# Attention scores and weighted sums written to PSUM instead of SBUF, and the count of earlier tokens per expert formed by TensorE instead of VectorE

## The reference, cut to what matters

```
W = weight * mask[None, :, :]                       # (16, 5000, 128)
h = einsum('bg,egp->bep', x, W) + bias              # (64, 16, 128)

scores = einsum('bhqd,bhkd->bhqk', q, k) * scale    # 8 heads of 16 + 2 dims, 16 positions
attn   = softmax(where(causal, scores, min))
out    = einsum('bhqk,bhkd->bhqd', attn, v)         # then @ W_o.T, added to h

top_scores, top_idx = top_k(sigmoid(xf @ gate_w.T), 2)
pos = cumsum(one_hot(flat_e, 64))[..., flat_e] - 1  # place of a token in its expert's list
y   = (silu(buf @ w1) * (buf @ w3)) @ w2            # per expert; routed = sum of the two, weighted
```

## Time and profile before

| What | Value |
|---|---|
| median of 3 runs | 318.57 us (317.5 to 321.41) |
| the profiled execution's own time | 316.17 us |
| its span, first to last instruction | 314.3 us |
| mean granted TensorE clock | 0.823 |
| busy: PE / DVE / ACT / POOL | 191.5 / 214.3 / 61.9 / 171.6 us |

### The profile page before, as it was taken

How to read it: one execution, slowest core, us unless ns; L and a number is a source line. 1 busy time by engine, 2 the same in 40 slices (tenths; PEclk the granted TensorE clock), 3 DMA queues, 4 the chain that set the end, 5 groups by cost and what they waited for, 6 DMA issues and landing times.

```text
span 314.3 us, 5301 instructions
## 1 busy us (share of the span) xinstructions
PE 191.5 (61%) x2106; PEld 154.3 (49%) x2106; DVE 214.3 (68%) x427; ACT 61.9 (20%) x167; POOL 171.6 (55%) x120
## 2 busy tenths in 40 slices
PE   0177509986765775774893693667177648999300
PEld 0177509774554554563673473542145537877200
DVE  0053289969899899899789869858829753374242
ACT  2030000020110110110020020112224743545300
POOL 2275495598669669669478478326105422003771
PEclk9999756999997997997797589555757986999755
DMA  8999999999954954853999000196910020824423
GB/s 277 255 418 411 424 368 406 416 418 417 396 198 144 333 189 152 332 180 146 305 219 234 15 1 19 32 209 202 243 24 10 8 67 19 237 69 117 117 58 78
DMA packets 32866, 64.14 MB, mean 204 GB/s; under 512 B 2858, under 2 KB 25351, under 8 KB 32391
## 3 DMA queue, kind: packets, MB, share of 16 engines
q1 hardware_dynamic: 31384, 59.47, 57.2%
q0 software_dynamic: 1024, 2.10, 2.4%
q10 hardware_dynamic: 432, 2.21, 1.8%
HBM read 55.91 MB, written 7.86 MB: 203 GB/s over the span
## 4 chain that ended last, share of the span: by engine, by line
DVE 48%; PE 18%; issue 10%; DMA 8%; SPq 5%; POOL 4%; ACT 3%; another core or an unknown queue 1%; DVEq 0%; POOLq 0%
DVE ring L964 8%; DMA ring<-in_L_tok_weight_dram 8%; DVE sc L994 6%; DVE o L1007 5%; DVE prod L984 3%; DVE prod L1004 3%; PE bank L656 3%; DVE sc L986 3%; PE bank L787 3%; POOL rstd L384 3%; PE bank L812 2%; SPq L301 2%; DVE qkn L976 2%; PE bank L697 2%; PE bank L797 2%
## 5 line engine op out<-in xcount | busy, mean ns | idle before, releaser
L395 POOL TENSOR_TENSOR ring<-ring,mask 128x896 f32<-128x896 f32 x48 | 104.7, 2202 | 21.0 <-DMA ring<-in_L_tok_weight_dram 20.9
L656 PE MATMUL bank<-ring,xT 128*64 128x128 f32 x1248 | 91.6, 310 | 33.5 <-POOL ring L395 29.2
L656 PEld LDWEIGHTS bank<-ring,xT 128*64 128x64 f32 x1248 | 82.0, 158 | 39.9 <-POOL ring L395 31.3
L964 DVE TENSOR_TENSOR ring<-ring,bank 128x1024 f32<-128x1024 f32 x24 | 29.1, 1213 | 31.1 <-DMA ring<-in_L_tok_weight_dram 30.9
L384 POOL TENSOR_TENSOR rstd<-mv,half 128x1 f32<-128x1 f32 (+1 forms) x24 | 18.3, 762 | 47.2 <-DVE mv L973 46.9
L415 POOL DMA_INDIRECT expert_inputs<-xf,scatter_index x16 | 21.8, 1364 | 32.0 <-DVE scatter_index L1072 29.5
L464 POOL DMA_INDIRECT ring<-expert_outputs,gather_index x16 | 16.0, 1001 | 26.3 <-DMA expert_outputs<-ring 22.1
L964 DVE TENSOR_TENSOR ring<-ring,mask 128x512 f32<-128x512 f32 x24 | 26.0, 1084 | 0.0
L994 DVE TENSOR_TENSOR sc<-sc,mx 128x16 f32<-128x16 f32 (+7 forms) x8 | 21.1, 2636 | 0.3
L1140 DVE TENSOR_TENSOR mask<-ring,bank 32x256 f32<-32x256 f32 (+1 forms) x24 | 10.0, 418 | 11.5 <-ACT ring L567 11.2
L1007 DVE TENSOR_REDUCE o<-prod 128x128 f32<-128x256 f32 (+7 forms) x8 | 16.5, 2063 | 0.0
(11 more groups left out here) (137 smaller groups left out, 300.0 us busy)
## 6 DMA issues: line engine op xcount, KB each, us to landing
ring<-in_L_tok_weight_dram SPq DMA_DIRECT2D x48, 832.0 KB, 8.9
ring<-expert_inputs SPq DMA_DIRECT2D x6, 512.0 KB, 5.8
expert_outputs<-ring SPq DMA_DIRECT2D x12, 256.0 KB, 2.8
mask<-in_L_tok_mask_dram SPq DMA_DIRECT2D x3, 832.0 KB, 15.1
expert_inputs<-prod ACTq DMA_DIRECT2D x2, 1024.0 KB, 11.4
w2p<-in_L_ffn_w_dram SPq DMA_DIRECT2D x2, 1024.0 KB, 10.3
w<-in_x_dram SPq DMA_DIRECT2D x1, 1250.0 KB, 12.4
expert_inputs<-ring SPq DMA_DIRECT2D x1, 1024.0 KB, 12.6
```

Of the source, the lines that this page charges most:

```text
L395: pool.tensor_tensor(unit(j, q, SPLIT, UC), unit(j, q, SPLIT, UC), mask[:, (m + SPLIT) * D:(m + UC) * D], ALU.mult).then_inc(s_pmask, 1)
L656: last = pe.matmul(bank[j % 2][64 * par:64 * par + 64, 0:D], xT[:, (UC * t + c) * B:(UC * t + c + 1) * B], unit(j, 2 * t + par, c, c + 1), ...
L964: dve.tensor_tensor(both(j, t, a, b), both(j, t, a, b), m.rearrange("p (u f) -> p u f", u=1).to_broadcast([P, 2, (b - a) * D]), ALU.mult). ...
```

## The change

The raw scores (written by L986 and the masking memset, read by L993 and L994) and the raw weighted sum (written by L1007, read by L1008) move from SBUF tiles to two stretches of PSUM bank 6, which PE uses for `turn_o` and `attend` at other times. `sc` keeps the shifted scores and the probabilities. Selections stay in one tile per chunk; the running sum and the wait on the rank before it are gone, and PE multiplies the matrix of ones with each earlier chunk's selection: for chunks 1 to 5 one to five matmuls instead of one, for chunk 7 one as before. The two totals per region before the last expert groups take 6 + 2 matmuls instead of 1 + 1.

```diff
-        o = sb("o", [P, 2, D])
+        o = sb("o", [P, D])
-        msel = sb("msel", [P, E], BF16)
+        msel = sb("msel", [P, NCH, E], BF16)
-        msum = sb("msum", [P, NCH, E], BF16)
+        raw, o_raw = bank[6][:, 0:S * NH], bank[6][:, P:P + D]
...
-                last = pe.matmul(bank[6][:, 448:448 + E], ltri[:], msel[:], start=True, stop=(j in (0, NCH1)))
-                if j not in (0, NCH1):
-                    pe.wait_ge(s_count, j)
-                    last = pe.matmul(bank[6][:, 448:448 + E], ones[:], msum[:, j - 1, :], start=False, stop=True)
+                first = 0 if j < NCH1 else NCH1
+                last = pe.matmul(bank[6][:, 448:448 + E], ltri[:], msel[:, j], start=True, stop=(j == first))
+                for i in range(first, j):
+                    last = pe.matmul(bank[6][:, 448:448 + E], ones[:], msel[:, i], start=False, stop=(i == j - 1))
...
-                then(dve.tensor_reduce(sc[:, 0, 0:n * NH], prod[:, 0:n * f].rearrange("p (s d) -> p s d", d=DK), AX.X, ALU.add))
-
-                then(dve.memset(sc[0:64, 0, (n - 1) * NH:n * NH], NEG))
+                then(dve.tensor_reduce(raw[:, 0:n * NH], prod[:, 0:n * f].rearrange("p (s d) -> p s d", d=DK), AX.X, ALU.add))
+
+                then(dve.memset(raw[0:64, (n - 1) * NH:n * NH], NEG))
...
-                sv = sc[:, 0, 0:n * NH].rearrange("p (s h) -> p s h", h=NH)
+                sv = raw[:, 0:n * NH].rearrange("p (s h) -> p s h", h=NH)
...
-                then(dve.tensor_reduce(o[:, 0, :], prod[:, 0:n * D].rearrange("p (s f) -> p f s", f=D), AX.X, ALU.add))
-                dve.tensor_tensor(o[:, 1, :].rearrange("p (h d) -> p h d", d=DH), o[:, 0, :].rearrange("p (h d) -> p h d", d=DH),
+                then(dve.tensor_reduce(o_raw, prod[:, 0:n * D].rearrange("p (s f) -> p f s", f=D), AX.X, ALU.add))
+                dve.tensor_tensor(o[:].rearrange("p (h d) -> p h d", d=DH), o_raw.rearrange("p (h d) -> p h d", d=DH),
...
-                if j >= 1:
-                    dve.wait_ge(s_rank, j)
-
-                dve.tensor_scalar(msel[:], bank[6][:, 384:384 + E], top[:, j, 1:2], None, ALU.is_ge).then_inc(s_sel, 1)
+                dve.tensor_scalar(msel[:, j], bank[6][:, 384:384 + E], top[:, j, 1:2], None, ALU.is_ge).then_inc(s_sel, 1)
                 dve.max_index(topi[:, j, :], top[:, j, :], bank[6][:, 384:384 + E]).then_inc(s_top, 1)
-                dve.wait_ge(s_sel, j + 1)
-                if j not in (0, NCH1):
-                    dve.wait_ge(s_count, j)
-                    dve.tensor_tensor(msum[:, j, :], msum[:, j - 1, :], msel[:], ALU.add).then_inc(s_count, 1)
-                else:
-                    dve.tensor_copy(msum[:, j, :], msel[:]).then_inc(s_count, 1)
```

More of the change, by code:

```diff
@@ L255, in tower_kernel @@
         s_xf, s_xfT, s_xfTs, s_gate = sem("xf"), sem("xf_transposed"), sem("xfT_copied"), sem("gate_logits")
-        s_sel, s_count, s_rank, s_slot, s_scat = (sem("selected"), sem("counted_before"), sem("ranked"), sem("slots"),
+        s_sel, s_rank, s_slot, s_scat = (sem("selected"), sem("ranked"), sem("slots"),
                                                   [sem("scattered_1"), sem("scattered_2")])
@@ L704, in turn_o @@
                     pe.wait_ge(s_slot, j)
-                pe.transpose(bank[6][:, 0:P], o[:, 1, :], ident).then_inc(s_oT, 1)
+                pe.transpose(bank[6][:, 0:P], o[:], ident).then_inc(s_oT, 1)
             def attend(j):
@@ L877, in _ @@
             pe.wait_ge(s_slot, NCH)
-            pe.wait_ge(s_count, NCH)
-            pe.matmul(bank[6][:, 0:E], ones[:], msum[:, NCH1 - 1, :], start=True, stop=True)
-            pe.matmul(bank[6][:, E:2 * E], ones[:], msum[:, NCH - 1, :], start=True, stop=True).then_inc(s_total, 1)
+            for r, js in enumerate((range(NCH1), range(NCH1, NCH))):
+                for j in js:
+                    last = pe.matmul(bank[6][:, E * r:E * r + E], ones[:], msel[:, j], start=(j == js[0]), stop=(j == js[-1]))
+            last.then_inc(s_total, 1)
             expert_steps(GROUPS1, GROUPS + 2)
```

## The result

| | Before | Changed |
|---|---|---|
| median of 4 runs each | 318.44 us (317.5 to 321.41) | 326.84 us (326.51 to 327.46) |
| ratio, 95% interval | | 1.0296 (1.0242 to 1.035) |
| the profiled execution's own time | 316.17 us | 326.85 us |
| its span; mean granted clock | 314.3 us; 0.823 | 325.1 us; 0.801 |

The change makes the kernel 3% slower. The forecast of 312 and its range of 307 to 321 missed; rival A, slower with 327 as a median, is what came. In the changed kernel `less_max`'s subtraction is L995 (L994 before), the product with the values L1005 (L1004), the division L1009 (L1008), the mask pieces L965 (L964), `add_attended` L1037 (L1036).

A forecast was written before the change was run, and what follows sets the result against it. Bound: a DVE, POOL and PE ring where DVE instructions with two SBUF inputs stand while POOL multiplies. 6.6 + 0.5 - 0.4 - 0.4 = 6.3 us off 316.17 gives 309.9, median 312; range 307 to 321.

The forecast's parts named there:

- rival A: L1004 stands through root and first pair, 4.7 us more; 8.3 us slower, 324.5, or 327 as median; chance 0.17.
- L994: Freed subtraction ends at 117.2, not 120.67; its wait moves to L1004, which goes at the third pair's end, 120.6.
- 6.6 + 0.5: Forecast gains in us: 6.6 summed over the rounds from freeing L994 and L1008, 0.5 from removing L1056 and L1058.
- PE's path: PE's sums, 3.71 us after the third pair, plus turn_o to attend, 2.09, make 5.8 and wouldn't hold up L1036.
- L1008 and L964: L1008 no longer waits; L1036 starts 7.26 us after the third pair with six positions, 7.53 with eight, 7.79 with ten.
- L1056: Its stand passes to the L964 piece behind; only its own end, 0.1 us in five rounds, is gained: 0.5.
- The last chunk: L994 takes 0.28 instead of 1.70 us, but a table load follows; nothing to 1.4 us gain, nothing taken.
- PE's matmuls with ones: Ten extra matmuls on the path cost 0.5 us if they pipeline, 2.4 if not; 0.4 taken.
- PSUM operands: Six DVE instructions with a PSUM side cost 0 to 2.9 us in all; 0.4 taken.
- Rival B: L1004 holds POOL back mid third pair, lengthening it 0.5 to 1.3 us; net 0 to 3 off; chance 0.25.
- Rival C: The PSUM operand doesn't free L994, which still stands; 316.5 us, or 319 as median; chance 0.05.

The follow-up runs named there:

- e2: Changed kernel with stats_h moved on DVE behind the value product, so POOL's root can't be ready early; ratio to before 0.9731.
- e4: Kernel before with only the raw scores moved to PSUM; ratio to before 1.0313.
- e9: Changed kernel with an already satisfied wait on POOL between scatter and third pair; one run, 327.68 us.
- e17: Changed kernel run again without any edit, in another set; ratio to before 1.0325.
- e8: Kernel before with only the raw weighted sum moved to PSUM; ratio to before 0.9779.
- e14: Kernel before with 16 superfluous matmuls on PE, four in each of chunks 1 to 4; ratio to before 0.9978.
- e3: Changed kernel with the probabilities in PSUM too, so the product reads one SBUF tile; ratio to before 0.9629.
- e13: Same program as e3, no edit, run in another set; ratio to before 0.9550.
- e10: Changed kernel with raw scores and weighted sum back in SBUF, leaving only the counting on TensorE; ratio to before 1.0102.
- e1: Changed kernel with the raw scores back in SBUF; ratio to before 0.9725.
- e11: Kernel before with scores, probabilities and weighted sum in PSUM, counting left on DVE; ratio to before 0.9579.
- e6: Changed kernel with POOL waiting for less_max between scatter and third pair, which makes it idle; ratio to before 1.0061.
- e5: Changed kernel with five POOL memsets replacing the loop's two indirect DMAs, scatters made behind the loop; one run, 320.47 us.
- e12: e3 with POOL's first pair held until heads is done on DVE; ratio to before 0.9738.
- e18: Same program as e3, no edit, run in another set; ratio to before 0.9743.

## Why the prediction was wrong, point by point

**The step that failed** stands under *L994*: "The wait moves to L1004. I take it that L1004 goes at 120.6, because L994 never got in before the pair's end in any round that has a scatter." The wait did move to L1004. But L994 went at the pair's end because nothing came behind: POOL was waiting for `stats_h`, which L994 itself held up. That was in the rows as the idle of 0.77, and rival A used it against itself ("there POOL had to wait for it"). The step took an outcome for a rule and missed that the removed stand was its cause. e2 shows it: the root made late again, the product goes at the pair's end, 3.86 us against 8.23. Its loop ends 8.3 us before the kernel before's (192.89 against 201.15), near the 6.6 + 0.5 that the prediction adds up on this step.

**Rival A** was right in mechanism and in the size of rounds: it gave 2.3 us more from third pair to `add_attended` with four positions, 2.7 with six, 1.9 with eight and ten; measured 2.5, 2.9, 2.1 and 2.2 (with six 132.58 - 121.78 against 7.90; eight 160.24 - 148.72 against 9.39; ten 188.90 - 176.70 against 9.98). At the loop's end it makes 8.5 us, and 7.2 at the flags, where A had 8.3. That the median matches A's 327 so closely is partly luck: between the profiled executions the difference is 10.7 us, since the tail adds 3.7 that stands in no sum, and the kernel before's profiled execution happened to lie 2.4 below its median where the changed one lies at its own. The idle of 0.77 spoke for more than 0.17.

**PE's path** was taken at one clock. "PE wouldn't hold this up" counts 3.71 us of sums and 2.09 from `turn_o` to `attend`, 5.8 in all. In e2, where the product goes as the prediction says, the same two parts take 3.93 and 3.32 us with the granted clock at 0.50, `add_attended` waits 1.27 us for PE and starts 7.2 after the pair. In the changed kernel, e4, e9 and e17 `attend` takes 0.80 us in all four rounds with four to ten positions; in the kernel before it took 0.49 with four and six. e8 and e14 have 0.80 there too, so the long idle of PE isn't the only thing that brings the lower level.

**L1008 and L964.** L1009 takes 0.29, as forecast. The sum behind it (7.26, 7.53 and 7.79 us to L1036) rests on the failed step. e3, where the product is out of the way, has 124.67 - 117.46 = 7.2 with six positions, against the forecast's 7.26, but that agreement is luck: DVE waits 0.94 us for PE there, at the lower clock. In e13, the same program with the clock at 1.00 from 121 to 125, it is 6.2.

**L1056.** Its stand went on to L965, 1.41 us at 112.12: nearly nothing gained alone (e10), as taken. e1 has this edit and e8's and is 6.2 us ahead of before at the flags, where e8 alone is 1.6 ahead: beside a loop that DVE sets, the time of L1056 may count. No run isolates that, and e3 against e11 shows nothing of it at the flags.

**The last chunk.** L995 takes 0.29 and the table load still comes 1.95 us after it (251.63 to 253.58): nothing gained, as taken.

**PE's matmuls with ones.** They pipeline, five in 0.46 us and eight in 0.40 (PE's timeline of the changed kernel):

```profile
220.06 0.46 PE L725 MATMUL bank<-msel,ones 128*128 128x64 bf16 x5
...
281.08 0.40 PE L880 MATMUL bank<-msel,ones 128*128 128x64 bf16 x8
```

So 0.4 us was right for them, and the tail's 3.6 was in no term. No row shown with the prediction has it.

**PSUM operands** cost nothing that shows: the subtraction takes 0.27 us with 112 numbers (226.52), where the undisturbed one in SBUF took 0.28, and the sum over positions that writes PSUM 3.69 us with 16 positions against 3.68 to SBUF. The rule of the Trainium skill, "VectorE: DVE Perf Modes", section on the TRN2 errata, that a PSUM source has the larger fixed cost, would have added an estimated 0.065 us each; these operations don't show it, though the scaling in the earlier trace rows does (0.402 against 0.343 us). The 0.4 us taken was too much and of no weight.

**Rival B**'s longer third pair came in e6 (4.82 us) and not in the changed kernel (4.11 to 4.13). **Rival C** is excluded: 0.21 us.

**The best version** has scores, probabilities and weighted sum in PSUM. With the counting on DVE it has 0.958 and 0.965, on TensorE 0.963, 0.955 and 0.974, the last where the idle was. Both beat the kernel before and the change.

## What to carry to other kernels

Before a standing instruction is freed, ask what its stand holds back on the other engine: here it delayed a root on POOL, and that gap let everything behind it on DVE in. Free the last instruction of such a chain together with the first (the product, not the subtraction alone), or leave the gap where it is. Take a stretch of PE's path at both levels of its clock before it is called no limit. And run the same program in two sets before a per cent in a stretch that the edit doesn't touch is put down to the edit.

## What the runs showed of the hardware

**A DVE instruction with two SBUF inputs can stand through several POOL instructions.** Behind an indirect DMA and with no idle since, it passed four boundaries between POOL's instructions (with ten positions three or four) in four rounds each of the changed kernel and e9 (8.0 to 8.9 us); behind memsets (e5) or behind an idle of 0.59 us or more (e1, e6, e12) it got in at the next one. The Trainium skill, "SBUF — State Buffer", section "Who interferes with whom", says of DVE's two-port modes that whoever issues first gets the shared pair "for the whole instruction" and the other blocks. The traces show the like for two-input instructions, in both directions: in e3 a DVE piece that takes 0.68 us alone is held for 4.27, and in e1, where DVE gets in, POOL's pair takes 4.56 us and not 4.10. **Open**: with twelve positions (4.47 us, the root 2.10) and in e6 with four (4.32 us, the root 1.05) the product got in between pair and root although an indirect DMA stood ahead and no idle is recorded. So the indirect DMA, or something that the memsets changed with it, is shown to matter, and the rule isn't complete.

**The freed instruction isn't slower for its PSUM side**, as shown above. **One program has two tails**, 30.34 us (e13) and 35.61 (e18); with the longer one goes an idle on ACT near the last expert steps that no edit here brings or takes away.
